# An attention layer with a quantised output: lengths by root and one Heron step on other engines, v turned by itself, the spread folded into the quantisation, and two steps of the bias network in another order

## The reference

```python
xn = ln(x, g_norm)
q = (xn @ Wq)                      # 16 heads of 64
k, v = (xn @ Wkv) split in two     # one head of 64, shared by all
k, v = concat(null key / value, k / v)
q = l2norm(q) * q_scale;  k = l2norm(k) * k_scale    # l2norm: t / max(norm(t), 1e-12)
sim = q @ k.T * 8 + bias           # bias: a small network of the distance i - j
sim = where(causal or masked, -max, sim)
o = softmax(sim) @ v
z = ln(o @ Wout, g_out)
act_scale = 127 / max(max(abs(z), axis=-1), 1e-5)
z_dq = clip(round(z * act_scale), -128, 127) / act_scale
result = x + z_dq @ ternary_weights.T + f_bias
```

## Time and profile before

| What | us |
|---|---|
| median of 3 runs | 1767.61 |
| lowest and highest of them | 1767.42, 1767.96 |
| profiled execution, its own time | 1767.12 |
| its span (first to last instruction) | 1765.3 |
| mean granted clock of TensorE | 0.968 of full |

### The profile page before, as it was taken

The page is one execution under the profiler, slowest core; times in us unless marked ns, Lnnn a source line. Parts: engine busy times, 40 slices in busy tenths (PEclk is TensorE's granted clock), DMA queues, the critical chain, the costliest instruction groups (busy, mean ns, idle before and its releaser), DMA issues.

```text
span 1765.3 us, 46353 instructions
## 1 busy us (share of the span) xinstructions
PE 1595.8 (90%) x15122; PEld 1075.9 (61%) x15122; DVE 1349.5 (76%) x2404; ACT 1163.3 (66%) x2228; POOL 1410.6 (80%) x923
## 2 busy tenths in 40 slices
PE   4876896999999999998995898799999999998997
PEld 2443554677777777775552555477777777776553
DVE  4335996888888888884764898788888888887576
ACT  4653554787788778777441555577887787787541
POOL 4653666999999999996662666799999999999574
PEclk9997998999999999998997999899999999999998
DMA  6001111012111111200122012021111112010022
GB/s 188 1 1 28 30 36 43 18 34 49 26 37 37 30 32 37 48 2 14 42 71 91 30 30 60 1 49 26 37 37 29 33 37 47 23 30 13 7 73 100
DMA packets 41304, 68.86 MB, mean 39 GB/s; under 512 B 8880, under 2 KB 9392, under 8 KB 41136
## 3 DMA queue, kind: packets, MB, share of 16 engines
q1 hardware_dynamic: 36512, 58.12, 13.5%
q10 hardware_dynamic: 4640, 8.54, 1.4%
HBM read 58.11 MB, written 8.54 MB: 38 GB/s over the span
## 4 chain that ended last, share of the span: by engine, by line
PE 43%; issue 23%; POOL 14%; DVE 9%; ACT 1%; DVEq 1%; POOLq 1%; DMA 0%; ACTq 0%; SPq 0%
PE ps L1222 21%; PE ps L1195 10%; PE ps L1198 9%; DVE work L981 5%; POOL rinv L516 4%; POOL work L521 4%; POOL work L548 3%; POOL work L566 2%; DVE work L1009 2%; PE ps L1264 1%; POOL rstd L511 1%; DVE denom L1006 1%; POOL work L523 1%; PE ps L1254 1%; PE ps L1177 0%
## 5 line engine op out<-in xcount | busy, mean ns | idle before, releaser
L536 POOL TENSOR_TENSOR work<-work 128x1024 f16<-128x1024 f32 (+2 forms) x576 | 977.6, 1730 | 44.6 <-ACT work L686 41.9
L981 DVE SCALAR_TENSOR_TENSOR work<-ps,tab 128x1024 f32<-128x1024 f32 (+3 forms) x640 | 668.2, 1058 | 139.9 <-PE ps L1198 137.7
L686 ACT ACTIVATE work<-work 128x1024 f32<-128x1024 f32 (+3 forms) x640 | 578.1, 924 | 206.9 <-DVE work L981 201.5
L1222 PEld LDWEIGHTS ps<-vals,work 128*128 128x128 bf16 (+1 forms) x8704 | 545.3, 98 | 115.8 <-POOL work L536 2.2
L1222 PE MATMUL ps<-vals,work 128*128 128x129 f16 x8704 | 600.6, 221 | 1.8 <-POOL work L536 1.8
L1195 PE MATMUL ps<-qo,kT 128*128 128x512 f16 (+3 forms) x1280 | 343.8, 350 | 21.0 <-DVE work L981 15.1
L1198 PE MATMUL ps<-qo,kT 128*128 128x512 f16 (+3 forms) x1280 | 341.6, 349 | 0.0
L1166 PE MATMUL ps<-wq,work 128*128 128x512 f16 x768 | 177.3, 389 | 19.9 <-DVE work L914 19.9
L1198 PEld LDWEIGHTS ps<-qo,kT 128*128 128x128 f16 x1280 | 123.1, 98 | 117.3 <-issue 2.8
L1264 PE MATMUL ps<-wout,work 128*128 128x512 f16 x768 | 172.5, 381 | 0.0
L1166 PEld LDWEIGHTS ps<-wq,work 128*128 128x128 f16 x768 | 74.4, 100 | 112.4 <-issue 32.7
(11 more groups left out here) (137 smaller groups left out, 1652.0 us busy)
## 6 DMA issues: line engine op xcount, KB each, us to landing
tab<-bias_table SPq DMA_DIRECT2D x64, 512.0 KB, 4.7
work<-in_x SPq DMA_DIRECT2D x32, 256.0 KB, 2.6
tab<-in_x SPq DMA_DIRECT2D x32, 256.0 KB, 2.8
out_x<-work ACTq DMA_DIRECT2D x32, 256.0 KB, 2.2
work<-in_L_cond_Wq SPq DMA_DIRECT2D x1, 2048.0 KB, 11.4
work<-in_L_cond_Wout SPq DMA_DIRECT2D x2, 1024.0 KB, 10.3
qo<-in_L_cond_w SPq DMA_DIRECT2D x1, 1024.0 KB, 7.3
qo<-in_L_cond_b SPq DMA_DIRECT2D x2, 256.0 KB, 5.6
```

Of the source, the lines that this page charges most:

```text
L536: pool.tensor_tensor(low[:, k % LRING, :, c0:512], probs[:, r, :, c0:512], high[:, r, :, c0:512], ALU.subtract).then_inc(low_pool, 1)
L686: act.activation(probs[:, k % RING, :, c0:512], probs[:, k % RING, :, c0:512], ACT.Exp).then_inc(expd, 1)
L981: dve.scalar_tensor_tensor(out=probs[:, k % RING, :, c0:512], in0=ps[:, 2 * (k % 2):2 * (k % 2) + 2, c0:512], scalar=SCORE, in1=tab[:, :, ...
L1222: last = pe.matmul(ps[:, sum_bank(i, q), (t % SUMS) * VS:(t % SUMS + 1) * VS], parts[:, rings[part], e, s * P:(s + 1) * P], vals[:, j, :], ...
```

## The change

Bias network: ScalarE's list has both copies ahead of the second layer's square. Setup: the mask is turned once by TensorE into `mask_r`, and the ones column of `vals` is written once for a batch.

Projections: the lengths come from ScalarE's square root of the scaled sums (`b_rootof`) and one Heron step on VectorE with five instructions on 17 elements; the guard against zero lies inside it (`LEAST`). GpSimd no longer has the power of the lengths, but k's gain. v is turned on its own (`b_turn_v`) out of the copied projection, before q and k and a step earlier, into another bank, and multiplied by the turned mask when it is stored. TensorE turns the next tile of x between the second and the third group of columns. ScalarE copies all of the turned q in one instruction. The null scores are gathered in `p_null`; one addition and one exponential per batch follow the last tile.

Output: the norm is the difference to the mean times the gain in one instruction of VectorE; 1/spread comes in with two of the small factors of `c_quant`. GpSimd's gain goes. `c_quant` has lag 3 instead of 4, y's turn, ternary product, final and store one lag less.

```diff
+LEAST = 1e-12 * WSCALE
+ROOT_SCALE = 0.25 * UNIT ** -2
...
-  def b_length(t, u):
-    pool.wait_ge(b_ssm, NT * b + t + 1)
-    pool.tensor_tensor(rinv[:, u, :], ssm[:, u, :], minus_half[:, :],
-            ALU.pow).then_inc(b_rinv, 1)
   def b_low(t, u):
-    pool.wait_ge(b_hi, 2 * (NT * b + t + 1))
+    pool.wait_ge(b_qn, NT * b + t + 1 + 2)
+    pool.wait_ge(b_hi, 2 * (NT * b + t + 1) - 2 + 2)
+    pool.tensor_tensor(kn[:, u, :], qn[:, u, H * DH:QKW], qk_scale[:, :], ALU.mult
+            ).then_inc(b_kn, 1)
+    pool.wait_ge(b_hi, 2 * (NT * b + t + 1) + 2)
     pool.tensor_tensor(q_part(u, 1), qn[:, u, 0:H * DH].rearrange("p (g e d) -> p g e d", e=2, d=DH),
...
             khl[:, u, 0:2, :], ALU.subtract).then_inc(b_lo, 1)
-  skewed(pool, NT, [(b_low, 4), (b_length, 3), (b_power, 0)],
-    tail=[(b_length, 3), (b_low, 4)])
+  skewed(pool, NT, [(b_low, 4), (b_power, 0)])
...
-  pool.wait_ge(b_pn, NT * (b + 1) + 2)
+  pool.wait_ge(b_pn, b + 1)
...
+    pool.wait_ge(c_as, NT * b + t + 1)
     pool.tensor_tensor(rstd[:, u, :], ve[:, u, :], minus_half[:, 0:1],
             ALU.pow).then_inc(c_rstd, 1)
-  def c_gain(t, u):
-    pool.wait_ge(c_zn, NT * b + t + 1 + 2)
-    pool.wait_ge(c_y1, NT * b + t + 1)
-    pool.tensor_tensor(y[:, u, :], zn, gout_b[:, :], ALU.mult).then_inc(c_y, 1)
   def c_resid(t, u):
...
     pool.tensor_tensor(xb[:, u, :], x_re[:, u, :], fbias_b[:, :], ALU.add).then_inc(c_xb, 1)
-  skewed(pool, NT, [(c_power, 3), (o_lows, 0), (c_gain, 3), (c_resid, 6)])
+  skewed(pool, NT, [(c_power, 3), (o_lows, 0), (c_resid, 5)])
...
-pipeline(NT, [(m_silu(1), 3), (m_silu(0), 1), (m_square(0), 0), (m_square(1), 2), (m_copy(1), 3),
-      (m_copy(0), 1), (w_high, 0)])
+pipeline(NT, [(m_silu(1), 3), (m_silu(0), 1), (m_square(0), 0), (m_copy(1), 3), (m_copy(0), 1),
+      (m_square(1), 2), (w_high, 0)])
...
-  def b_q(t, u):
-    g = NT * b + t
-    act.wait_ge(b_v, g + 1)
-    act.wait_ge(b_qn, g + 1)
-    act.wait_ge(b_snp, g + 1)
-    for n, w in enumerate((512, 512, REST)):
+  def b_q(n):
+    def f(t, u):
+      g = NT * b + t
+      w = (512, 512, REST)[n]
+      if n == 0:
+        act.wait_ge(b_qn, g + 1)
+      elif n == 2:
+        act.wait_ge(b_vT, g + 1)
+        act.wait_ge(b_snd, g + 1)
       act.wait_ge(b_proj, 3 * g + n + 1 + 6)
       act.copy(q_sb[:, u, 512 * n:512 * n + w], ps[:, 1 + n, 0:w]).then_inc(b_qc, 1)
+    return f
   def b_square(t, u):
...
     act.activation(sq, q_sb[:, u, 0:QKW], ACT.Square).then_inc(b_sq, 1)
+  def b_rootof(t, u):
+    g = NT * b + t
+    act.wait_ge(b_ss, g + 1 + 1)
+    act.wait_ge(b_rinv, g + 1)
+    act.activation(root[:, u, :], ss[:, u, :], ACT.Sqrt, scale=ROOT_SCALE).then_inc(b_root, 1)
   def b_high(t, u):
     g = NT * b + t
...
     act.wait_ge(b_turned, g + 1)
     act.copy(q_part(u, 0), qn[:, u, 0:H * DH].rearrange("p (g e d) -> p g e d", e=2, d=DH)
         ).then_inc(b_hi, 1)
-    act.wait_ge(b_kn, g + 1)
+    act.wait_ge(b_kn, g + 1 + 2)
     act.copy(khl[:, u, 0:2, :], kn[:, u, :].unsqueeze(1).to_broadcast([P, 2, DH])
         ).then_inc(b_hi, 1)
...
     g = NT * b + t
     act.wait_ge(b_turned, g + 1 + 2)
     act.wait_ge(table_stored, 16)
-    act.copy(qT[:, 0:8, bass.ds(t * P, P)],
-        ps[:, 4, :].bitcast(F16).rearrange("p (h r) -> p h r", r=P)).then_inc(b_ca, 1)
-  def b_null(t, u):
-    g = NT * b + t
-    act.wait_ge(b_snd, g + 1 + 1)
-    act.activation(p_null[:, bass.ds(t, 1), :].squeeze(1), sn[:, u, :], ACT.Exp
-          ).then_inc(b_pn, 1)
-  skewed(act, NT, [(b_q, 3), (b_xt, 2), (b_square, 3), (b_high, 4), (b_turn, 5), (b_null, 5)])
+    act.copy(qT[:, :, bass.ds(t * P, P)],
+        ps[:, 4:6, :].rearrange("p a c -> p (a c)").bitcast(F16).rearrange("p (h r) -> p h r", r=P)
+        ).then_inc(b_ca, 1)
+  skewed(act, NT, [(b_q(0), 3), (b_q(1), 3), (b_xt, 2), (b_q(2), 3), (b_square, 3), (b_high, 4),
+          (b_rootof, 3), (b_turn, 5)])
+  act.wait_ge(b_sall, b + 1)
+  act.activation(p_null[:, :, :], p_null[:, :, :], ACT.Exp).then_inc(b_pn, 1)
...
-  skewed(act, NT, [(o_highs, 0), (c_turn, 1), (c_yturn, 5), (store, 8)], after_first=store_last)
+  skewed(act, NT, [(o_highs, 0), (c_turn, 1), (c_yturn, 4), (store, 7)], after_first=store_last)
...
-dve.tensor_scalar(maskf[:, :], mask8[:, :], 1.0 / WSCALE, None, ALU.mult).then_inc(setup_chain, 1)
+dve.tensor_scalar(maskf[:, :], mask8[:, :], 1.0 / WSCALE, None, ALU.mult).then_inc(mask_ready, 1)
+dve.wait_ge(mask_mm, 1)
+dve.tensor_copy(mask_r[:, :], ps[:, 7, 64:64 + B * NT]).then_inc(mask_ready, 1)
+dve.wait_ge(mask_ready, 2)
 with dve.Fori(0, B) as b:
-  dve.memset(q_sb[:, :, PROJ:PROJ + 1], WSCALE).then_inc(ones_set, 1)
-  dve.wait_ge(ones_set, b + 1)
+  dve.tensor_scalar(vals[:, :, 2 * DH:VS].rearrange("p t o -> p (t o)"), mask_r[:, bass.ds(b * NT, NT)],
+          WSCALE, None, ALU.mult).then_inc(ones_set, 1)
...
     dve.wait_ge(b_sq, g + 1)
+    dve.wait_ge(b_rinv, g + 1)
     dve.tensor_reduce(ss[:, u, :], sq.rearrange("p (h d) -> p h d", d=DH), AX.X, ALU.add
             ).then_inc(b_ss, 1)
-    dve.wait_ge(b_ss, g + 1 + 1)
-    dve.tensor_scalar(ssm[:, u, :], ss[:, u, :], 1e-24 * WSCALE ** 2, UNIT ** -2, ALU.max,
-            ALU.mult).then_inc(b_ssm, 1)
   def b_unit(t, u):
     g = NT * b + t
-    dve.wait_ge(b_qc, 3 * g + 3 + 3)
-    dve.wait_ge(b_turned, g + 1)
-    dve.tensor_scalar(v_mask[:, u, :], q_sb[:, u, V0:PROJ + 1],
-            maskf[:, bass.ds(g, 1)], None, ALU.mult).then_inc(b_v, 1)
-    dve.wait_ge(b_rinv, g + 1)
+    dve.wait_ge(b_root, g + 1)
+    dve.wait_ge(b_rinv, g + 2)
+    dve.scalar_tensor_tensor(out=root_m[:, :], in0=root[:, u, :], scalar=LEAST * ROOT_SCALE ** 0.5,
+                in1=root[:, u, :], op0=ALU.max, op1=ALU.max).then_inc(b_near, 1)
+    dve.wait_ge(b_near, 4 * g + 1)
+    dve.reciprocal(near[:, :], root_m[:, :]).then_inc(b_near, 1)
+    dve.wait_ge(b_near, 4 * g + 2)
+    dve.scalar_tensor_tensor(out=quot[:, :], in0=ss[:, u, :], scalar=LEAST ** 2, in1=near[:, :],
+                op0=ALU.max, op1=ALU.mult).then_inc(b_near, 1)
+    dve.wait_ge(b_near, 4 * g + 3)
+    dve.scalar_tensor_tensor(out=twice[:, :], in0=quot[:, :], scalar=ROOT_SCALE, in1=root_m[:, :],
+                op0=ALU.mult, op1=ALU.add).then_inc(b_near, 1)
+    dve.wait_ge(b_near, 4 * g + 4)
+    dve.wait_ge(b_qn, g + 1)
+    dve.wait_ge(b_snd, g + 1)
+    dve.reciprocal(rinv[:, u, :], twice[:, :]).then_inc(b_rinv, 1)
+    dve.wait_ge(b_rinv, g + 1 + 2)
     dve.wait_ge(b_lo, 2 * g + 2)
+    dve.wait_ge(b_kn, g + 1)
     dve.tensor_tensor(qn[:, u, :].rearrange("p (h d) -> p h d", d=DH),
...
             ).then_inc(b_qn, 1)
-    dve.wait_ge(b_qn, g + 1 + 2)
-    dve.tensor_tensor(kn[:, u, :], qn[:, u, H * DH:QKW], qk_scale[:, :], ALU.mult
-            ).then_inc(b_kn, 1)
-    dve.wait_ge(b_snd, g + 1)
-    dve.tensor_tensor(sn_part[:, :], q_sb[:, u, QKW:V0], rinv[:, u, 0:H], ALU.mult
-            ).then_inc(b_snp, 1)
-    dve.wait_ge(b_snp, g + 1 + 2)
-    dve.wait_ge(b_pn, g + 1)
-    dve.scalar_tensor_tensor(out=sn[:, u, :], in0=sn_part[:, :], scalar=SCORE,
-                in1=null_shift[:, :], op0=ALU.mult, op1=ALU.add
-                ).then_inc(b_snd, 1)
+    dve.tensor_tensor(p_null[:, bass.ds(t, 1), :].squeeze(1), q_sb[:, u, QKW:V0], rinv[:, u, 0:H],
+            ALU.mult).then_inc(b_snd, 1)
   def b_turn(t, u):
     g = NT * b + t
     dve.wait_ge(b_turned, g + 1 + 2)
-    dve.wait_ge(table_stored, 16)
-    dve.tensor_copy(vals[:, bass.ds(t, 1), 0:DH].squeeze(1), ps[:, 6, 2 * P:2 * P + DH]
-            ).then_inc(b_vh, 1)
-    dve.tensor_copy(qT[:, 8:16, bass.ds(t * P, P)],
-            ps[:, 5, :].bitcast(F16).rearrange("p (h r) -> p h r", r=P)
-            ).then_inc(b_cd, 1)
     dve.tensor_copy(kT[:, :, bass.ds(t * P, P)],
             ps[:, 6, 0:2 * P].rearrange("p (a r) -> p a r", r=P)
             ).then_inc(b_cd, 1)
-    dve.tensor_copy(vals[:, bass.ds(t, 1), 2 * DH:VS].squeeze(1),
-            ps[:, 6, 2 * P + DH:2 * P + VW]).then_inc(b_cd, 1)
-    dve.wait_ge(b_vh, g + 1)
-    dve.tensor_tensor(vals[:, bass.ds(t, 1), DH:2 * DH].squeeze(1), ps[:, 6, 2 * P:2 * P + DH],
-            vals[:, bass.ds(t, 1), 0:DH].squeeze(1), ALU.subtract).then_inc(b_cd, 1)
-  skewed(dve, NT, [(b_xlow, 2), (b_unit, 4), (b_sum, 3), (b_turn, 5), (b_norm, 1), (b_stat, 0)])
+  def b_values(t, u):
+    g = NT * b + t
+    dve.wait_ge(b_vT, g + 1 + 2)
+    v = ps[:, 7, 0:DH]
+    dve.tensor_scalar(vals[:, bass.ds(t, 1), 0:DH].squeeze(1), v, mask_r[:, bass.ds(g, 1)], None, ALU.mult
+            ).then_inc(b_vh, 1)
+    dve.wait_ge(b_vh, g + 1 + 1)
+    dve.scalar_tensor_tensor(out=vals[:, bass.ds(t, 1), DH:2 * DH].squeeze(1), in0=v,
+                scalar=mask_r[:, bass.ds(g, 1)],
+                in1=vals[:, bass.ds(t, 1), 0:DH].squeeze(1), op0=ALU.mult,
+                op1=ALU.subtract).then_inc(b_vl, 1)
+  skewed(dve, NT, [(b_unit, 4), (b_norm, 1), (b_values, 4), (b_xlow, 2), (b_turn, 5), (b_sum, 3), (b_stat, 0)])
+  dve.wait_ge(b_snd, NT * (b + 1) + 2)
```

(76 more changed lines are left out.)

41 lines of the change are left out of this document (21 added, 20 removed).

## The result

The changed kernel takes 1716.22 us (median of four runs, 1715.05 to 1716.59) against 1767.78 (1767.42 to 1768.09) for the kernel before, timed beside it: ratio 0.9706, 95% interval [0.9695, 0.9718]. Its profiled execution took 1716.0 us with a span of 1714.2; before it was 1767.12 and 1765.3. The forecast was 1722.4, the range 1708 to 1744. So the gain was 51.1 us from one profiled execution to the other, where 44.7 were forecast.

What follows compares the result with a forecast made beforehand. TensorE bounds attention, left untouched; projections wait on GpSimd and VectorE, the network step on ScalarE's copy, output on TensorE and its ends. Network -11.1, mask +1.0, projections -25.0, output -9.6: -44.7 on 1767.12 gives 1722.4 us; range 1708 to 1744.

Steps and rivals of the forecast that it cites:

- Network: Bias network: copies ahead of the second square make a step 5.82 us instead of 6.80; 11.1 us gained over sixteen steps.
- split step: Bias network: in the four steps with a wq split the copies come about 1.15 us late in the new order.
- Mask: Before the first statistics: turning the mask once loses 1.0 us, between 0.5 and 1.5.
- TensorE's loop: Projections: turns put before the third part remove TensorE's wait and leave its floor of 7.8 us a tile.
- floor of 7.8: Projections: TensorE's own work in a tile, without waiting, is about 7.8 us.
- TensorE's rival: Projections: they run at TensorE's 7.8 us a tile, 1714.6 us in all; chance 0.2.
- Root and Heron step: Projections: lengths leave GpSimd for ScalarE and VectorE; 8.1 us a tile, 10.4 gained over 13 periods, 1.1 in the first two steps.
- loop over two tiles: Projections: projection, third copy, square, GpSimd's line 521, VectorE's chain and back to TensorE; 16.2 us for two tiles.
- Tail: Last tile's projection to first score: 24.1 us instead of 25.1, 1.0 gained per batch.
- Output: Ends of the output stages: 5.1 us gained at the first and 4.5 at the very end, together 9.6.
- The port: Projections: small two-input operations meet GpSimd one after another; 8.6 us a tile, 1735.4 us or 1743; chance 0.15.
- The slower rival: Projections: if root and square or copy share no table, two loads make ScalarE's loop 9.7 us per tile, 1774; chance 0.03.

Runs made afterwards that it cites:

- e2: Changed kernel with both of the network's copies also ahead of the first square: 1718.16 us, ratio 0.9719.
- e4: Changed kernel without the guard on the root: 1710.18 us, ratio 0.9673.
- e10: Changed kernel with the guard moved from VectorE into the bias of ScalarE's root: 1710.19 us, ratio 0.9672.
- e13: Changed kernel with one more GpSimd operation of 128 elements ahead of its low half of q in each tile: 1725.28 us, ratio 0.9753.
- e9: Changed kernel with the null score's sum and exponential taken tile by tile, so two table loads more per tile: 1732.43 us, ratio 0.9798.
- e6: Changed kernel with the output's stage lags and VectorE's stage order put back, folded spread kept: 1723.31 us, ratio 0.975.

## Why the prediction was right, and where its sizes were off

From one profiled execution to the other the parts came out so (forecast beside it): network and mask -10.2 (-10.1); projections of both batches -31.1 (-25.0); attention +0.3 (0), all in the second batch; output stages -10.0 (-9.6); hand-over between the batches -0.2 (0). The sign and the mechanism of each part held; 6.1 of the missing 6.4 us are in the projections. That the first pair agrees so well is luck: 1.2 of the 10.2 us lie ahead of the first whole step, where the traces vary, and without them network and mask gave 9.0.

1. *Network.* Step 5.80 (5.82), split step 6.83 (5.82 + 1.15 = 6.97). Forecast 11.1; undone, it is 10.2. The forecast counted sixteen steps. Between the second and the last group of first-layer matmuls are fourteen: ten gained 1.0 us each, the four with the late copy nothing (6.82 before), 9.9 in all (95.2 to 85.3). The copy's delay in the split steps is real, but it isn't a pure loss: taken away, it comes back as a late SiLU (e2).

2. *Mask.* 6.08 us from the last bias row to the first statistics, before 4.98: 1.1 (1.0).

3. *TensorE's loop.* The wait ahead of the turn of x is gone as forecast. The floor of 7.8 was too high: TensorE waits 2.7 us in ten tiles of 7.96, so its own work is at most 7.7; in the last two periods of the kernel without a guard, with no wait at all, it took 7.55. "For it: only about 0.3 us lie between the two loops" was right in kind; but TensorE's rival was never reached, even at a pair of 15.64 us it still waited 0.13 a tile (1.3 us in ten tiles of the kernel without a guard).

4. *Root and Heron step.* This is the term that was mis-sized. The loop over two tiles was named rightly, down to GpSimd's line; e4, e10 and e13 show it from both sides (0.36 less and 0.51 more a pair for what was taken from it or put into it). Forecast 16.2 us, measured 16.00 in the walk above and in the pairs on either side of it. The sum held errors that nearly cancel. Its terms add up to 16.35, not 16.2; 0.4 us for GpSimd's second operation "to get out of the way" was not paid, since the operation behind the guard is a reciprocal and runs beside it (206.19 and 214.13), projection to third copy was 7.03, not 7.3, and the guard ended 0.04 behind GpSimd's operation, not 0.2; against that, the four small operations and the gap ahead of the units took 1.25 us, not 0.8. A pair 0.2 us shorter is 0.1 a tile; over 13 periods, 115.7 became 103.5, 12.2 gained (10.4). The second batch did the same within 0.2 us. The first two steps gained 1.4 (1.1, though its own two terms, 0.75 and 0.45, make 1.2); most of that is the first tile, which varies by as much with the clock.

5. *Tail.* 23.5 us (24.1): 1.6 gained for 1.0, and 2.0 in the second batch, where it had been 25.55. That the stalls behind GpSimd's low half "mostly go" was wrong: in the last tile of both batches the guard starts inside line 523 and takes 1.76 us, for 0.2 where nothing holds it, so most of the stall of 1.8 us only moved from the units to it. Which other terms of the tail were too dear in return was not taken apart. Of table loads the forecast said "two more"; there are four more, eight in all. The two more are those for the root, once a batch, in its first tile, with ScalarE idle around them: a miss that cost nothing. A load of 1.28 us was right. By the drain of the Trainium skill ("ScalarE: Activation LUTs", section "What ACT_TABLE_LOAD costs") the tail would have been 0.4 us longer than before; the trace has the load 0.02 us behind the copy, for 1.28 us, and the exponential right behind it, here and in all tiles of e9. The measurement decides: no drain is seen.

6. *Output.* First end 5.1 gained (5.1), second 4.9 (4.5), and the extra tile ahead of the last projection costs 1.5 (1.1), of which the first end is already net. e6 gives the lags 7.1 us of it.

*The rivals.* The port did not take the gain, though the wait is there: from 150 to 250 us the guard takes 0.72 us on average, where the operation of the same kind behind it takes 0.19; but it begins while line 523 runs and ends with it, and line 523 is in the loop anyway. What the guard keeps back is the step behind it, 0.36 us a pair, as e4 and e10 show. The slower rival was priced too high. Its ScalarE loop, "7.0 us with its forced waits becomes 9.7 per tile", came out at 8.72: the forced waits are air that a load can fill. The prediction had it decide for slower from a loop of 8.9 up, and 8.72 is below that. With two loads in every tile (e9) the kernel ran 1732.43 us, not 1774: even then it is not slower than before. Between root and square, the pair that it named, no load stands in any trace.

## What to carry to other kernels

When an instruction waits in a chain over two engines, ask which kind it is: a guard moved into the bias of the root let a reciprocal stand where a two-input operation had stood, and gave 6 us for 0.09 us of ScalarE. Work with no deadline of its own, like a batch's one exponential with its table load, belongs in the idle time ahead of the last turn and not behind it. Price a rival's added work against the idle time of its engine, not against its busy time plus the waits: two table loads and an exponential more a tile on ScalarE, 2.8 us, cost 0.7.

## What the runs showed of the hardware

- VectorE's reciprocal of 17 elements takes 0.27 us while GpSimd runs its 128x1024 subtraction; operations with two inputs from SBUF (17 elements) started in it end 0.03 us behind it: 0.99 us at 205.16, 0.69 at 203.18. The Trainium skill, "SBUF — State Buffer", section "SBUF: two separate sides", has the rule that an operation of VectorE with two SBUF inputs and a GpSimd operation that reads SBUF exclude each other for a whole instruction; the traces agree, and show that the length of the small operation doesn't matter. Line 924 of the kernel before, with one tensor input, was held alike (1.73 us, ending 0.03 behind line 521), so two inputs are not the only case.
- A table load right behind a copy starts after 0.01 to 0.02 us and takes 1.28, and the function behind it starts 0.01 to 0.02 us later.
- A bias operand makes ScalarE's root of 17 elements 0.31 us instead of 0.22.
- At the hand-over TensorE's clock falls: in the windows of the changed kernel it is granted 1.00 from 194 to 258 us and 0.50 (1.2 GHz) from 269.5 to 277.7, where TensorE was busy 4.20 of 8.20 us behind a wait of 3.9 us. The sixteen turns of q then take 1.89 us instead of 1.06. No run here tried to keep the clock up. The first tile of a batch pays for it again: 8.73 to 10.27 us, by when the clock comes back.

```profile
194.00:258.00 64.00, 61.87 (x485) 38.49 (x482) 56.38 (x125) 49.90 (x73) 27.82 (x31) 1.00 0.22 58
...
269.50:277.70 8.20, 4.20 (x36) 3.67 (x36) 2.77 (x9) 3.04 (x4) 2.82 (x3) 0.50 0.00 0
```
